# GpSimd held back behind VectorE's two-input operations, slot by slot, in a chunked state-space block on one Trainium2 core

## The reference, cut to what matters

```
xi, z = split(x @ in_proj_w.T);  xc = silu(conv1d(xi, 4 taps) + conv_b)
delta = softplus((xc @ x_proj_w.T)[0] * dt_w + dt_b);  B, C = (16 states each)
for each chunk of 128 positions, for each state s of 16:
    A_bar = exp(delta * A_s);  log_A_cum = cumsum(log(max(A_bar, 1e-10)))
    A_cum = exp(min(log_A_cum, 80)); wcum = cumsum(delta*B_s*xc / max(shift(A_cum), 1e-10))
    h = A_cum * wcum / max(A_bar, 1e-10) + h_last * A_cum
    y += C_s * h
y = (y + D * xc) * silu(z);  out = y @ out_proj_w.T
```

## Time and profile before

| what | us |
|---|---|
| median of 3 runs (6332.12 to 6334.46) | 6333.33 |
| the profiled execution | 6330.54 |
| its span, first to last instruction | 6328.8 |
| TensorE busy | 5738.2 (91%) |
| VectorE busy | 5610.6 (89%) |
| ScalarE busy | 4340.1 (69%) |
| GpSimd busy | 3416.7 (54%) |

### The profile page before, as it was taken

How to read it: one execution, slowest core, us unless ns; L and a number is a source line. 1 busy time by engine, 2 the same in 40 slices (tenths; PEclk the granted TensorE clock), 3 DMA queues, 4 the chain that set the end, 5 groups by cost and what they waited for, 6 DMA issues and landing times. The chain is left out here.

```text
span 6328.8 us, 77654 instructions
## 1 busy us (share of the span) xinstructions
PE 5738.2 (91%) x16088; PEld 2692.3 (43%) x16152; DVE 5610.6 (89%) x6545; ACT 4340.1 (69%) x5130; POOL 3416.7 (54%) x2139
## 2 busy tenths in 40 slices
PE   5999999999989999999898999998999999989998
PEld 2444444444444444444444444444444444444443
DVE  4899899999998998899889989988999889988997
ACT  4776766677667767676666667766766767667665
POOL 2555555555555555555555555555555555555554
PEclk8999999999999999999999999999999999999998
DMA  1111121121111211211212112111121121111210
GB/s 63 11 16 18 14 17 16 14 19 15 14 18 14 16 16 14 18 15 14 18 13 17 16 14 19 15 14 18 13 16 16 16 17 15 14 18 13 17 14 14
DMA packets 158033, 105.38 MB, mean 17 GB/s; under 512 B 121008, under 2 KB 121008, under 8 KB 157488
## 3 DMA queue, kind: packets, MB, share of 16 engines
q1 hardware_dynamic: 157488, 100.71, 17.5%
HBM read 42.63 MB, written 16.78 MB: 9 GB/s over the span
## 5 line engine op out<-in xcount | busy, mean ns | idle before, releaser
L509 POOL TENSOR_TENSOR acc<-acc,term 128x1024 f32<-128x1024 f32 x512 | 1374.3, 2684 | 2626.9 <-DVE term L1403 2626.9
L1053 PE MATMUL state<-sources,tri_upto 128*128 128x512 f32 x4096 | 2064.0, 628 | 426.9 <-DVE term L1395 426.1
L1043 PE MATMUL cum<-step,tri_before 128*128 128x512 f32 x4096 | 1977.6, 606 | 58.3 <-POOL step L486 54.8
L744 ACT ACTIVATE decay<-cum,neg_a 128x1024 f32<-128x1024 f32 x1024 | 1137.3, 1111 | 1244.2 <-PE cum L1043 1244.2
L1395 DVE SCALAR_TENSOR_TENSOR term<-state,crow,decay 128x1024 f32<-128x1024 f32 x1024 | 1309.5, 1279 | 508.2 <-PE state L1053 391.6
L1053 PEld LDWEIGHTS state<-sources,tri_upto 128*128 128x128 f32 x4096 | 765.9, 196 | 1318.0 <-issue 1237.2
L1377 DVE SCALAR_TENSOR_TENSOR sources<-cum,brow,dx 128x1024 f32<-128x1024 f32 x1024 | 1303.7, 1273 | 14.8 <-ACT cum L760 12.5
L486 POOL TENSOR_SCALAR step<-delta,limit 128x1024 f32<-128x1024 f32 x1024 | 1288.9, 1265 | 24.5 <-PE cum L1043 22.6
L1043 PEld LDWEIGHTS cum<-step,tri_before 128*128 128x128 f32 x4096 | 799.5, 198 | 1098.8 <-issue 1032.8
L936 PE MATMUL fbank<-win,xnT 128*128 128x512 f32 x2048 | 978.5, 601 | 32.2 <-ACT xi L611 24.7
L1240 DVE SCALAR_TENSOR_TENSOR conv<-xiT,cw,conv 128x128 f32<-128x128 f32 x1536 | 948.9, 678 | 20.9 <-ACT conv L640 15.3
(11 more groups left out here) (130 smaller groups left out, 4457.0 us busy)
## 6 DMA issues: line engine op xcount, KB each, us to landing
hfirst<-hrows SPq DMA_DIRECT2D x496, 64.0 KB, 3.9
xt<-in_x SPq DMA_DIRECT2D x64, 256.0 KB, 2.7
hrows<-term SPq DMA_DIRECT2D x1024, 4.0 KB, 1.6
xres<-in_x SPq DMA_DIRECT2D x64, 256.0 KB, 2.7
out_x<-xres SPq DMA_DIRECT2D x64, 256.0 KB, 2.2
gate_last<-gate SPq DMA_DIRECT2D x512, 0.5 KB, 2.0
win<-in_w_in SPq DMA_DIRECT2D x2, 2048.0 KB, 10.8
hrows<-hrows SPq DMA_DIRECT2D x64, 64.0 KB, 2.3
```

The lines of the kernel that those rows point to most:

```text
L509: nc.gpsimd.tensor_tensor(sums, sums, term[term_at(s - 1)][:, :], ALU.add).then_inc(added, 1)
L744: nc.scalar.activation(decay[s % 4][:, :], cum[s % 2][:, :], ACT.Exp, scale=neg_a[:, s:s + 1]).then_inc(decay_ready, 1)
L1043: last = nc.tensor.matmul(cum[s % 2][:, cols], tri_before[:, :], step[s % 2][:, cols], start=True, stop=True)
L1053: last = nc.tensor.matmul(state[:, cols], tri_upto[:, :], source[s % 2][:, cols], start=True, stop=True)
```

## The change

Only GpSimd's program changes. Before the work of each slot it waits (`turn`) for a count that VectorE reaches at the end of the slot before: in most slots that of its last operation there with two SBUF inputs (or of the last one of the slot). Within a slot the order becomes: in odd slots from 3 on the pair's addition first (of pair s-2, so each addition stands one slot later than before), then `limit_sum`, then `limit_step`. Slot 14's `skip` stays last in its slot.

```diff
+AFTER_FRONT = {5: "tap1a", 6: "tap0b", 7: "halo_out", 10: "dt_lin", 11: "under", 12: "log1p", 13: "delta", 14: "dx"}
...
+            def turn(t, s, more, more2):
+
+                prev, nxt = t.shift(-1), t.shift(1)
+                prev2 = prev.shift(-1) if prev is not None else None
+                if s == 0:
+                    if prev2 is not None:
+                        pool.wait_ge(end_dve, at(END_DVE, prev2, "inv"))
+                elif s == 1:
+                    pool.wait_ge(carry_in, t.n + 1)
+                elif s == 3 and prev2 is not None:
+                    pool.wait_ge(end_dve, at(END_DVE, prev2, "out"))
+                elif s == 4 and prev is not None:
+                    pool.wait_ge(end_dve, at(END_DVE, prev, "fixg"))
+                elif s == 8 and more2:
+                    pool.wait_ge(norm_dve, at(NORM_DVE, t.shift(2), "var_eps"))
+                elif s == 15 and prev is not None:
+                    pool.wait_ge(end_dve, at(END_DVE, prev, "rstd"))
+                elif s in AFTER_FRONT and more:
+                    pool.wait_ge(front_dve, at(FRONT_DVE, nxt, AFTER_FRONT[s]))
+                else:
+                    pool.wait_ge(source_ready, slot_at(t, s))
+
             def body(t, more, more2):
                 prev, nxt = t.shift(-1), t.shift(1)
                 for s in range(NS):
+                    turn(t, s, more, more2)
+                    if s > 2 and s % 2:
+                        add_pair(t, s - 2)
+                    if s + 2 < NS and s + 2 in ROOM_POOL:
+                        limit_sum(t, s + 2)
+                    if more and s + 2 >= NS and s + 2 - NS in ROOM_POOL:
+                        limit_sum(nxt, s + 2 - NS)
                     if s + 3 < NS:
                         limit_step(t, s + 3)
                     elif more:
                         limit_step(nxt, s + 3 - NS)
-                    if s + 2 < NS and s + 2 in ROOM_POOL:
-                        limit_sum(t, s + 2)
-                    if more and s + 2 >= NS and s + 2 - NS in ROOM_POOL:
-                        limit_sum(nxt, s + 2 - NS)
                     if s == 0 and prev is not None:
                         add_pair(prev, NS - 1)
                         finish(prev)
-                    if s > 0 and s % 2 == 0:
-                        add_pair(t, s - 1)
                     if more:
                         if s == 14:
                             skip(nxt)
```

## The result

| | before | after |
|---|---|---|
| median, us | 6333.9 (4 runs) | 6013.49 (4 runs, 6012.23 to 6017.92) |
| ratio, 95% interval | | 0.9495 (0.9478 to 0.9511) |
| span of the profiled execution | 6328.8 | 6012.7 |
| TensorE, VectorE busy | 5738.2, 5610.6 | 5669.0, 4947.0 |
| ScalarE, GpSimd busy | 4340.1, 3416.7 | 4341.9, 3370.9 |

The kernel is 5.0% faster, 320 us; 5998 us were forecast. VectorE's busy time fell by 664 us though its 6545 instructions are the same: that was waiting after the start, counted as work.

The account below looks back on a forecast made before the run. TensorE and VectorE taking turns, with VectorE's taps blocked by GpSimd, were taken to bound it; 12.66 + 3.6 - 4.4 - 1.2 - 0.2 = 10.5 us per pass, x 32 = 335 us, gave 5998 us, range 5880 to 6110 (52%).

Parts of the forecast that it names:

- What bounds the kernel: TensorE and VectorE take turns; VectorE's taps in slots 4 and 6, blocked by GpSimd, make TensorE stand still.
- Taps freed: Slots 4 to 7: GpSimd starts after the taps, all four TensorE stalls go; +12.66 us per pass.
- clock: TensorE's clock, seen lower after the long stalls, recovers once they go; +3.6 us per pass (0 to 5.7).
- new wait at slot 8: Slot 7 to 8: TensorE waits 1.5 us for step 10, `proj` 0.7 more; -4.4 us per pass.
- Slots 3, 9, 11, 13: VectorE operations there still meet a step, 0.7 to 1.8 us each, but fillers cover it; 0 (down to -2).
- one us to spare: Slot 3: step 6 comes after 4.6 us and is needed 5.6 us after the slot's start.
- Slots 14, 15 and 0: `skip` holds up slot 14's pair, then step 2 comes 1.2 us late for TensorE; net -1.2 us per pass.
- The loop's turn: Once per pass VectorE's idle 3.4 us stays; ScalarE's `xi` behind it may come 0.2 later; -0.2 us.
- Slower: Rival, 11%: step late in every odd slot, each delay feeding the next; 6450 us at 1.25 us late each.
- Half of it is given back on VectorE: Rival, 18%: moved GpSimd operations block pair, slot 5's taps, `gate`, log1p and `dx` beyond the fillers; about 6160 us.
- the signs: Taps near 2.2 us (slot 5: 3.3), `term` wait under 100, `step` wait 150 to 250, clock 0.98 to 0.99, among others.

Follow-up runs that it names:

- the fill: Kernel before, GpSimd's pair additions replaced by a memset of the same accumulator with zeros, which writes SBUF and reads nothing: 5908.69 us (one run).

## Why the prediction was right, point by point

- **What bounds the kernel.** Right: TensorE and VectorE in turns, late in slots 4 and 6 through blocked taps. Shown by two waits alone bringing 285 us, and by the fill.
- **Taps freed, +12.66; clock, +3.6; new wait at slot 8, -4.4.** Together 11.9 per pass; slots 4 to 8 gave 12.8 - 1.0 = 11.8. The mechanisms came as forecast: no listed wait is left in slots 4 to 6; step 10 was forecast 1.5 us late and `proj` 0.7, measured 1.59 and 0.58. That the sum fits to 0.1 is luck, for two terms were too small by about as much. The kernel with slot 7's addition moved shows them apart. Without the new wait slots 4 to 8 take 17.5 us less than before, where 16.3 were counted, and the new wait costs 5.7 where 4.4 were counted: 4.7 in slot 7, and 1.0 in slot 8 for a lower clock behind it, which the sum put at nothing.
- **Slots 3, 9, 11, 13, put at 0.** Mis-sized: -1.0 per pass, in slots 3 and 11. The sum had VectorE blocked there and GpSimd on time. It is the reverse: VectorE's `gate` and log1p go through at 1.2 us, `room` (slot 3; 2.15 in slot 11) takes 2.16 us instead of 1.11, and the step behind it comes some 0.25 us late for `cum`. GpSimd, slot 3:

```profile
2968.80 2.36 POOL L510 TENSOR_TENSOR acc<-acc,term 128x1024 f32<-128x1024 f32 x1 [6.09 <-DVE xres L1392]
2971.14 2.16 POOL L498 TENSOR_SCALAR room<-total,limit 128x1024 f32<-128x1024 f32 x1
2973.29 1.11 POOL L487 TENSOR_SCALAR step<-delta,limit 128x1024 f32<-128x1024 f32 x1
```

  Step 6 ends at 2974.40 and `cum` starts at 2974.45; the "one us to spare" was the 1.05 that `room` lost. Where `step` stands ahead of `room`, or without the fourteen waits, slots 3 and 11 take the 19.1 us of before.
- **Slots 14, 15 and 0, -1.2.** Measured -0.8. `skip` did start before the pair, by 0.20 us where 0.3 was counted, and `state` was late by 0.42 to 0.45; step 2 was late by 0.58 to 0.66 us instead of 1.2, because VectorE's `xn`, which the sum let it meet in full, started just ahead of the step (3042.43) and cost it 0.28 us.
- **The loop's turn, -0.2.** Within 0.1 of nothing.
- **The rivals.** "Slower", with every odd slot late, did not come: two of eight were late by over 0.3 us. "Half of it is given back on VectorE" came nearer in amount than in kind: 18.1 us per pass of TensorE's lost time went and 7.9 came anew, but only the 1.2 of slot 14 through a late `term`; the rest came through GpSimd's late `step` and `room`. The order's own share (113 us without any wait) was in none of them; it did not show in the sum because in the changed kernel the waits free the same taps. Of the signs, TensorE's wait for `step` came in at 143.1 us, just under the 150 to 250 named, and the others as named.

## What to carry to other kernels

When an engine's busy time hides blocking, compare the same operation in different places: eight equal taps of 2.2, 6.0 and 6.9 us name the cause before any wait table does. Let the engine that shares the ports start its work behind the other's two-input operations, and put first in each burst what the bounding engine waits for; where the addition stood was worth 177 us, more than half as much as all sixteen waits and the new order (320). Guard only the places whose delay isn't covered: two of sixteen waits gave nearly everything, and a wait where the delay was covered can cost half of what another one earns, as in slots 3 and 11.

## What the runs showed of the hardware that was not expected

The lock was expected; how little decides it was not. `skip` starts 0.20 us ahead of the pair and goes through in 2.36 us, and the pair waits it out (3.23 for 1.22). In slot 11 VectorE's log1p starts 0.05 us ahead of `room`, and there `room` waits (2.15 for 1.11). (In slot 3 a small VectorE copy begins 0.09 us ahead of `room`, and `gate` goes through behind it.)

```profile
3018.59 1.21 DVE L1300 SCALAR_TENSOR_TENSOR xi<-acc,xi 128x1024 f32<-128x1024 f32 x1
3018.64 2.15 POOL L498 TENSOR_SCALAR room<-total,limit 128x1024 f32<-128x1024 f32 x1
```

The waits of 1.59 and 0.58 us in slot 7 were followed by a lower clock in 17 of the loop's 58 tiles, always in the second tile of a pass, and not in the others. One such stretch of `state` behind them, and one of 4.8 us ahead (share of TensorE's clock in the column PEclk):

```profile
core 0: us, PE busy (x) PEld busy (x) DVE busy (x) ACT busy (x) POOL busy (x), PEclk, DMA share, GB/s
2992.00:2996.80 4.80, 3.27 (x8) 1.06 (x6) 4.58 (x6) 1.94 (x2) 4.53 (x3) 1.00 0.48 69
3001.20:3004.60 3.40, 3.40 (x7) 1.34 (x7) 0.00 (x0) 3.25 (x7) 2.56 (x2) 0.54 0.00 0
```
